# One more expert tile in the ramp, a new order of its work, and router products of 120 columns

## Chip, core and metric

One core of one Trainium2 chip runs one launch of the kernel. The metric is the device time of that launch in microseconds (us); less is better. The engines are named as in the profile: PE (TensorE matmul), PEld (its weight load), DVE (VectorE), ACT (ScalarE), POOL (GpSimd) and SP (SyncE, which issues most DMAs).

## What is computed

x has 2 batches of 2048 tokens of 256 numbers, all float32. After a layer norm, two branches work on the same rows, and their product is added to x:

```python
xn = _layernorm(x, axis=-1)
s = _L0_attn_ref(xn, ...)          # q, k, v, gate: xn @ W; delta rule over 2048 tokens; @ Wo
g = _silu(_L0_ffn_ref(xn, ...))    # 8 experts, each token goes to the one of its largest logit
x = x + s * g

# in the attention branch, 4 heads, keys of 128, values of 64
k = k * rsqrt(sum(k * k) + 1e-12);  beta = sigmoid(xn @ Wb)
delta = (v_t - einsum('bhk,bhkv->bhv', k_t, S)) * b_t;  S = S + k_t delta;  o_t = q_t S
o = o * rsqrt(mean(o * o) + 1e-5) * norm_w * silu(xn @ Wg)
# in the expert branch
logits = xn @ router_w.T;  expert = argmax(softmax(logits))
out = square(relu(xn @ expert_fc[e])) @ expert_proj[e].T
```

## The kernel before

**Tiles.** The tokens of each batch make 16 chunks (c) of 128 rows. One chunk is two row tiles, one of each batch (b = 0, 1), and eight states (2 batches by 4 heads). The attention branch goes chunk by chunk, since the state S is carried on. Its frontend for chunk a is K, Q and VG (products of `xT` with `wk_sb`, `wq_sb`, `wvg_sb`), the transposes kT, the Gram products G and the products PTm. The inverse of a triangular matrix is built in six levels: M0, then for each level l the products L, Dm and T, each waiting on a result that DVE (`Pm_`, `dM`) or ACT (`dZ`) writes from the product before; F and Zc close it. KS, U, O, dS, `ogT_` and `wo` then carry the state through the chunk. Products that need more than float16 are three float16 products of high and low parts (`pairs`).

**Experts.** The rows are sorted by expert into 39 tiles of 128 rows. A tile needs its rows, gathered from `xn_d` in DRAM by POOL (`rows(j)`), and the two weights of its expert (`load_weights(j)`, SP, 2 MB). `experts(n)` issues the next n of a stream of units, 16 to a tile: eight with `fcw` (L461), eight with `pjw` (L472), and the transposes of the next tile's rows (L444) inside them. Buffers ring over three tiles.

**Routing.** `logits_of(c)` multiplies the chunk by `wbr_sb`, which holds the 4 columns for beta and the 8 of the router: 12 moving columns, four float32 products for a chunk, which the trace shows as 8 matmuls. Chunks 0 and 1 (EARLY) go to one bank, the rest to another. When all 16 chunks have logits, ACT copies them (`logits_rest`), DVE makes one-hots of them (`choose`, `count`), PE ranks them (`ranks`, L402 and L404, and `counts`), DVE pads the counts (`pad_counts`), PE adds offsets (`places`), DVE turns that into places (`place_rows`), and into one-hots of rows and of tiles (`tiles_onehot`, `rows_onehot(0)`, `rows_onehot(1)`, `tile_numbers`, and `tile_rows` on ACT), PE multiplies these (`tokens_of_rows`, L431), and DVE writes `from_row` and `to_row` (`keep_tokens`). `past_tiles`, `experts_of_tiles` and `keep_experts` name each tile's expert, `tile_e`; SP waits for that before the first expert weights (L328) and for `keep_tokens` before the third.

**Order.** Each engine runs its own list, written out by hand, in order; semaphores join them. There is a ramp, 14 steps and a tail. The ramp normalises x (loads in five parts, X_PARTS; `stats_of`, `variance` on DVE, `rstd_of` on POOL, `normal` on ACT and DVE), transposes it (`turn(c)` on PE, `keep_xT(c)` on ACT), routes, does the frontend of chunks 0 and 1, the levels of chunk 0 and FIRST_TILES expert tiles. Step i does the recurrence of chunk i-1, the levels of chunk i and the frontend of chunk i+1, with three expert tiles (`step3`) or two (`step2`); STEPS lists them. PE's ramp begins with 64 products of zeros (`warm_up`, L372). A step begins on PE with KS, and on DVE with `R32` (L1518). The tail does the last two tiles and chunk 15, multiplies by the experts' output and adds x.

Of the kernel before, what the change touches and what calls it, by code (L numbers as in the profile page):

```python
# [29 lines left out]
P = 128  # L30
# [36 lines left out]
def build_program(nc, x, wq, wk, wvg, wbr, wo, norm_w, fc, pj, out):  # L67
    with ExitStack() as ctx:
# [19 lines left out]
        FIRST_TILES, STEPS = 1, [3] * 8 + [2] * 6  # L88
# [199 lines left out]
        with nc.Block() as block:  # L288
            @block.sync
            def _(sp):  # L290
# [12 lines left out]
                load_w(wbr_sb, wbr, wbr_in)  # L303
                load_w(wk_sb, wk, wk_in)
                load_x(1)
                load_w(wq_sb, wq, wq_in)
                load_w(wvg_sb, wvg, wvg_in)
                for k in range(2, len(X_PARTS)):
                    load_x(k)
# [50 lines left out]
            def _(pe):  # L360
# [26 lines left out]
                def logits_of(c):  # L387
                    pe.wait_ge(xT_ok, c + 1)
                    if c == 0:
                        pe.wait_ge(wbr_in, 16)  # L390
                    for b in range(B):
                        o = lg_first[:, 2 * c + b, :] if c < EARLY else lg_rest[:, 2 * (c - EARLY) + b, :]
                        for k in range(KC):
                            ins = pe.matmul(o, xT[:, c, b, k, :], wbr_sb[:, k, :], start=(k == 0), stop=(k == KC - 1))  # L394
                    ins.then_inc(lgp, 1)

# [283 lines left out]
                def ramp():  # L680
# [3 lines left out]
                    logits_of(0)  # L684
                    logits_of(1)
                    turn(2)
                    turn(3)
                    K(0, 0)
                    logits_of(2)
                    logits_of(3)  # L690
                    Q(0, 0)
                    turn(4)
                    turn(5)
                    K(0, 1)
# [7 lines left out]
                    Q(0, 1)  # L702
                    logits_of(7)
                    logits_of(8)
                    turn(10)
                    turn(11)
                    logits_of(9)
                    turn(12)
                    VG(0, 0)
                    logits_of(10)  # L710
                    turn(13)
                    logits_of(11)
                    turn(14)
                    logits_of(12)
                    logits_of(13)
                    turn(15)
                    kT(0, 0)
                    logits_of(14)
                    logits_of(15)
                    G(0, 0)  # L720
                    kT(0, 1)
                    PTm(0, 0)
                    VG(0, 1)
                    G(0, 1)
                    ranks()
                    counts()
                    M0(0)
                    places()
                    Q(1, 0)
                    L(0, 0)  # L730
                    K(1, 0)
                    Dm(0, 0)
                    Q(1, 1)
# [39 lines left out]
                    PTm(1, 0)  # L773
                    experts(3)
# [164 lines left out]
            def _(act):  # L939
# [121 lines left out]
                def ramp():  # L1061
                    normal(0)
                    normal(1)
                    keep_xT(0)
                    normal(2)
                    keep_xT(1)
                    normal(3)
                    keep_xT(2)
                    keep_xT(3)
                    ksq_(0, 0)  # L1070
                    logits_first()
                    normal(4)
# [7 lines left out]
                    ksq_(0, 1)  # L1080
# [8 lines left out]
                    q_h(0, 1)  # L1089
# [14 lines left out]
                    M0c(0, 0)  # L1104
                    M0c(0, 1)
                    q_h(1, 0)
                    dZ(0, 0, 0)
                    q_h(1, 1)
                    dZ(0, 0, 1)
                    tile_rows()  # L1110
# [23 lines left out]
                    dZf_(0, 1)
                    keep_y(0)
                    y_sigmoid(0)
                    keep_rows(1)
# [136 lines left out]
            def _(dve):  # L1274
# [309 lines left out]
                def ramp():  # L1584
# [4 lines left out]
                    normal(1)  # L1589
# [602 lines left out]
```

## Time and profile before

| | us |
|---|---|
| three timed runs | 813.15, 813.34, 815.94 |
| their median | 813.34 |
| the profiled execution, its own time | 815.19 |
| span of the profiled execution, first to last instruction | 813.4 |
| PE busy in that span | 773.4 (95%) |
| PE weight loads | 655.9 (81%) |
| DVE, POOL, ACT busy | 529.8, 391.0, 346.9 |
| mean granted clock of PE | 0.966 |

The profiled time is 1.8 us more than its span. All times of rows count from the start of the span. A timeline row gives start, duration, engine, line, operation, the tiles written and read, the shape, and how many instructions are merged in it (xN); in brackets stands the idle time before it and who ended it. Matmuls are pipelined, so the start of the next row, not the duration, tells what a group of them took.

### The profile page before, as it was taken

To read this page: it belongs to the slowest core of one execution; us is meant where nothing else is said; L and a number is where in the kernel's file an instruction comes from. 1 tells how busy PE (TensorE), PEld (TensorE's weight loads), DVE (VectorE), ACT (ScalarE), POOL (GpSimd) and SP (SyncE) were. 2 spreads that over 40 slices of the span, in tenths; PEclk is the share of its full clock that TensorE was granted. 3 is DMA by queue.
4 is the path that set the end of the run, shared out by engine and by line. 5 is a ranking of instruction groups with operands and counts; after the bars stand their busy time and mean duration, and the time that the engine had idled before them with its cause. 6 is when DMAs were issued, how large, how long until landed. Compare 5 with 4: busy or idle time off the path is not lost.

```text
span 813.4 us, 22106 instructions
## 1 busy us (share of the span) xinstructions
PE 773.4 (95%) x8970; PEld 655.9 (81%) x8970; DVE 529.8 (65%) x1159; ACT 346.9 (43%) x754; POOL 391.0 (48%) x407
## 2 busy tenths in 40 slices
PE   6997899999999999999999999999999999999953
PEld 5874788888888889888888888878787878788842
DVE  5568575655756556575665746776767676777587
ACT  3823334444443445344444444444443534344420
POOL 5512473545626364363544625463647464554421
PEclk9969899999999999999999999999999999999965
DMA  9505534424343263333533343232333323140087
GB/s 299 197 11 222 213 118 166 186 112 164 135 170 125 111 212 139 118 124 145 206 112 130 135 175 147 112 124 112 124 111 118 118 110 127 62 172 10 21 275 249
DMA packets 37748, 116.25 MB, mean 143 GB/s; under 512 B 3664, under 2 KB 24400, under 8 KB 27664
## 3 DMA queue, kind: packets, MB, share of 16 engines
q1 hardware_dynamic: 33904, 104.62, 35.3%
q0 software_dynamic: 3744, 10.23, 3.9%
q8 instruction: 72, 1.18, 0.6%
q14 instruction: 28, 0.23, 0.1%
HBM read 101.33 MB, written 13.50 MB: 141 GB/s over the span
## 4 chain that ended last, share of the span: by engine, by line
PE 88%; DVE 4%; POOL 3%; DMA 2%; issue 2%; ACT 1%; another core or an unknown queue 1%; POOLq 0%; DVEq 0%; SPq 0%
PE bank L461 18%; PE bank L472 16%; PE bank L505 7%; PE bank L537 7%; PE bank L490 7%; PE bank L435 4%; PE bank L437 4%; PE bank L436 4%; PE bank L676 4%; PE bank L572 3%; PE bank L582 3%; PE bank L592 2%; PE bank L517 2%; POOL ImM L2043 2%; PE bank L394 2%
## 5 line engine op out<-in xcount | busy, mean ns | idle before, releaser
L472 PE MATMUL bank<-wts,hT 128*128 128x256 f32 x624 | 173.0, 394 | 0.0
L461 PE MATMUL bank<-xsT,wts 128*128 128x128 f32 x1248 | 167.9, 282 | 0.2
L461 PEld LDWEIGHTS bank<-xsT,wts 128*128 128x128 f32 x1248 | 151.8, 193 | 11.0 <-issue 11.0
L1495 DVE TENSOR_TENSOR Pm<-bank,lvl_mask 128x256 f16<-128x256 f32 x192 | 72.6, 419 | 70.4 <-PE bank L572 69.4
L1038 ACT CAST Z<-bank 128x256 f16<-128x256 f32 x192 | 63.5, 376 | 120.8 <-PE bank L592 120.7
L2024 POOL TENSOR_TENSOR XTl<-f_t,XTh 128x512 f16<-128x512 f32 x32 | 40.1, 1261 | 154.7 <-DVE XTh L1438 154.7
L472 PEld LDWEIGHTS bank<-wts,hT 128*128 128x128 f32 x624 | 104.7, 191 | 6.8
L1506 DVE TENSOR_TENSOR M<-bank,M 128x256 f16<-128x256 f32 x192 | 73.4, 418 | 56.3 <-PE bank L582 54.9
L982 ACT ACTIVATE hT<-bank 128x512 f32<-128x512 f32 x78 | 46.7, 598 | 51.3 <-PE bank L461 51.0
L537 PE MATMUL bank<-wvg_sb,xT 128*128 128x512 f32 x128 | 65.1, 633 | 0.3 <-DVE gate L1457 0.3
L505 PE MATMUL bank<-xT,wq_sb 128*128 128x128 f32 x512 | 64.0, 279 | 0.0
L490 PE MATMUL bank<-wk_sb,xT 128*128 128x512 f32 x128 | 62.3, 609 | 0.0
L505 PEld LDWEIGHTS bank<-xT,wq_sb 128*128 128x128 f32 x512 | 61.1, 194 | 0.4
L2043 POOL TENSOR_TENSOR ImM<-ident,M 128x512 f32<-128x512 f16 x32 | 38.1, 1212 | 45.4 <-DVE M L1506 45.4
L582 PEld LDWEIGHTS bank<-Pm,Z 128*128 128x128 f16 x768 | 35.2, 99 | 24.3 <-issue 13.1
L1997 POOL TENSOR_TENSOR y_sb<-y_sb,y_sg 128x256 f32<-128x256 f32 x39 | 29.7, 763 | 48.3 <-ACT y_sg L1001 48.1
L986 ACT ACTIVATE hT<-hT 128x512 f32<-128x512 f32 x78 | 49.3, 633 | 1.1
L2018 POOL TENSOR_TENSOR k16l<-f_t,k16h 128x512 f16<-128x512 f32 x32 | 38.1, 1206 | 24.0 <-DVE k16h L1424 24.0
L1431 DVE TENSOR_TENSOR f_t<-bank,up_neg 128x512 f32<-128x512 f32 x32 | 21.9, 684 | 39.6 <-PE bank L437 39.2
L592 PEld LDWEIGHTS bank<-ident,M 128*128 128x128 f16 x768 | 35.1, 99 | 14.3 <-DVE M L1506 4.0
L1477 DVE COPY M<-ident 128x512 f16<-128x512 f16 x32 | 21.0, 656 | 38.0 <-PE bank L437 34.0
L2001 POOL DMA_INDIRECT y_d<-y_sb,to_row x39 | 41.6, 1066 | 8.7 <-issue 5.3
(213 smaller groups left out, 1957.7 us busy)
## 6 DMA issues: line engine op xcount, KB each, us to landing
wts<-in_fc SPq DMA_DIRECT2D x39, 1024.0 KB
wts<-in_pj SPq DMA_DIRECT2D x39, 1024.0 KB
wts<-in_x SPq DMA_DIRECT2D x10, 512.0 KB, 9.6
wts<-y_d SPq DMA_DIRECT2D x4, 1024.0 KB, 9.2
out_x<-wts SPq DMA_DIRECT2D x16, 256.0 KB, 2.3
xn_d<-wts SPq DMA_DIRECT2D x3, 1024.0 KB, 4.4
x_first<-in_x SPq DMA_DIRECT2D x4, 512.0 KB, 12.1
wts<-in_x SPq DMA_DIRECT2D x4, 256.0 KB, 4.0
```

Of the source, the lines that this page charges most:

```text
L461: ins = pe.matmul(psum[bank[n]][:, (c % 4) * P:(c % 4 + 1) * P], fcw[r][:, k, c * P:(c + 1) * P], xsT[:, k, :], start=(k == 0), stop=(k == ...
L472: ins = pe.matmul(psum[bank[0]][:, 0:D], hT[:, c, :], pjw[r][:, c, :], start=(c == 0), stop=(c == HC - 1))
L490: ins = pe.matmul(psum[KG_BANK[b]][:], xT[:, a, b, k, :], wk_sb[:, k, :], start=(k == 0), stop=(k == KC - 1))
L505: ins = pe.matmul(bank4(QV_BANK)[:, h, :], wq_sb[:, k, h * DK:(h + 1) * DK], xT[:, a, b, k, :], start=(k == 0), stop=(k == KC - 1))
L537: ins = pe.matmul(psum[QV_BANK][:], xT[:, a, b, k, :], wvg_sb[:, k, :], start=(k == 0), stop=(k == KC - 1))
L582: ins = pe.matmul(half4(b)[:, h, :], Z[:, H * b + h, :], Pm[:, H * b + h, :], start=True, stop=True)
L592: ins = pe.matmul(half4(b)[:, h, :].rearrange("p (n c) -> p n c", c=s), M[:, H * b + h, :], evens(ident16[:].unsqueeze(1), s, 1)[:, 0], st ...
L986: act.activation(half(n), half(n), ACT.Square).then_inc(sq_ok[n], 1)
L1038: act.copy(evens(h4(Z, b), s, 1), half4(b).rearrange("p h (n c) -> p h n c", c=s)).then_inc(dZ_ok[b], 1)
L1495: dve.tensor_tensor(h4(Pm, b).rearrange("p h (n c) -> p h n c", c=s), half4(b).rearrange("p h (n c) -> p h n c", c=s), mask, ALU.mult).the ...
L1506: dve.tensor_tensor(evens(h4(M, b), s), half4(b).rearrange("p h (n c) -> p h n c", c=s), evens(h4(M, b), s), ALU.add).then_inc(dM_ok[b], 1)
L2043: pool.tensor_tensor(h4(ImM, b), ident16[:].unsqueeze(1).to_broadcast([P, H, P]), h4(M, b), ALU.subtract).then_inc(ImM_ok[b], 1)
```

## The change

The lists of PE, ACT, DVE and POOL in the ramp are written anew; `step3`, `step2`, the tail and all other operations stay as they are. The ramp issues two expert tiles instead of one, and one of the three-tile steps becomes a two-tile step. Parts 1 to 4 of x move ahead in SP's queue: part 1 ahead of `wk`, parts 2 and 3 ahead of `wq`, part 4 ahead of `wvg`. A router product streams the 12 columns of `wbr_sb` ten times, as a broadcast, and writes 120 columns of its bank, of which the first 12 are kept; the 108 others are written over by later chunks or not read.

The diff, without indentation in the lists of calls; what is cut moves the rest of the frontend of chunk 1 and of the levels of chunk 0 on ACT, DVE and POOL to match the list of PE, which is whole.

```diff
--- before.py
+++ after.py
@@ -85,7 +85,7 @@
         EARLY = 2
         WARM_UP = 64
         X_PARTS = [range(0, 2), range(2, 4), range(4, 8), range(8, 12), range(12, 16)]
-        FIRST_TILES, STEPS = 1, [3] * 8 + [2] * 6
+        FIRST_TILES, STEPS = 2, [3] * 7 + [2] * 7
         assert FIRST_TILES + sum(STEPS) + 2 == NT
 
 
@@ -301,12 +301,13 @@
         load_x(0)
         load_w(wbr_sb, wbr, wbr_in)
+        load_x(1)
         load_w(wk_sb, wk, wk_in)
-        load_x(1)
+        load_x(2)
+        load_x(3)
         load_w(wq_sb, wq, wq_in)
+        load_x(4)
         load_w(wvg_sb, wvg, wvg_in)
-        for k in range(2, len(X_PARTS)):
-            load_x(k)
         load_w(wo_sb, wo, wo_in)
         sp.dma_start(nw_sb[:], norm_w).then_inc(wo_in, 16)
         xn_v = xn_d.rearrange("(q p) d -> p q d", p=P)
@@ -389,10 +390,14 @@
             if c == 0:
                 pe.wait_ge(wbr_in, 16)
             for b in range(B):
-                o = lg_first[:, 2 * c + b, :] if c < EARLY else lg_rest[:, 2 * (c - EARLY) + b, :]
+                bank, q = (RANK_BANK, 2 * c + b) if c < EARLY else (LG_BANK, 2 * (c - EARLY) + b)
+                o = psum[bank][:, q * (H + E):(q + 10) * (H + E)].rearrange("p (r n) -> p r n", r=10)
                 for k in range(KC):
-                    ins = pe.matmul(o, xT[:, c, b, k, :], wbr_sb[:, k, :], start=(k == 0), stop=(k == KC - 1))
+                    ins = pe.matmul(o, xT[:, c, b, k, :], wbr_sb[:, k, :].unsqueeze(1).to_broadcast([P, 10, H + E]),
+                                    start=(k == 0), stop=(k == KC - 1))
             ins.then_inc(lgp, 1)
         def ranks():
             pe.wait_ge(consts, C_ROUTE)
@@ -682,16 +687,16 @@
 turn(0)
 turn(1)
 logits_of(0)
+K(0, 1)
 logits_of(1)
 turn(2)
+K(0, 0)
 turn(3)
-K(0, 0)
+Q(0, 0)
+turn(4)
 logits_of(2)
 logits_of(3)
-Q(0, 0)
-turn(4)
 turn(5)
-K(0, 1)
 logits_of(4)
 turn(6)
 turn(7)
@@ -699,79 +704,79 @@
 turn(8)
 logits_of(6)
 turn(9)
-Q(0, 1)
 logits_of(7)
 logits_of(8)
 turn(10)
+logits_of(9)
+kT(0, 1)
+kT(0, 0)
 turn(11)
-logits_of(9)
 turn(12)
-VG(0, 0)
+turn(13)
 logits_of(10)
-turn(13)
+turn(14)
 logits_of(11)
-turn(14)
+G(0, 1)
+G(0, 0)
+turn(15)
 logits_of(12)
 logits_of(13)
-turn(15)
-kT(0, 0)
 logits_of(14)
 logits_of(15)
-G(0, 0)
-kT(0, 1)
+Q(0, 1)
 PTm(0, 0)
-VG(0, 1)
-G(0, 1)
 ranks()
 counts()
+places()
+K(1, 0)
+VG(0, 0)
+PTm(0, 1)
 M0(0)
-places()
-Q(1, 0)
 L(0, 0)
-K(1, 0)
+tokens_of_rows()
+experts_of_tiles()
 Dm(0, 0)
-Q(1, 1)
+VG(0, 1)
 T(0, 0)
 L(0, 1)
 Dm(0, 1)
-experts_of_tiles()
+Q(1, 0)
 T(0, 1)
+K(1, 1)
+L(0, 2)
+transpose_rows(0)
+Q(1, 1)
+experts(1)
+Dm(0, 2)
+experts(5)
+T(0, 2)
+experts(4)
+L(0, 3)
+experts(2)
+kT(1, 0)
+Dm(0, 3)
+experts(4)
+T(0, 3)
 VG(1, 0)
-PTm(0, 1)
-L(0, 2)
-tokens_of_rows()
-Dm(0, 2)
-VG(1, 1)
-T(0, 2)
-K(1, 1)
-L(0, 3)
-Dm(0, 3)
-transpose_rows(0)
-T(0, 3)
-experts(1)
-L(0, 4)
-experts(2)
-Dm(0, 4)
-experts(2)
-T(0, 4)
-experts(2)
-L(0, 5)
-experts(2)
-Dm(0, 5)
 experts(1)
 kT(1, 1)
+L(0, 4)
+experts(3)
+Dm(0, 4)
+G(1, 0)
+G(1, 1)
+T(0, 4)
+experts(3)
+L(0, 5)
+experts(4)
+Dm(0, 5)
+VG(1, 1)
 T(0, 5)
-experts(1)
-kT(1, 0)
+PTm(1, 0)
+PTm(1, 1)
 F(0)
-G(1, 1)
-experts(1)
-G(1, 0)
+experts(5)
 Zc(0)
-PTm(1, 1)
-experts(1)
-PTm(1, 0)
-experts(3)
@@ -1062,22 +1067,21 @@
 normal(0)
 normal(1)
 keep_xT(0)
+keep_xT(1)
 normal(2)
-keep_xT(1)
 normal(3)
+ksq_(0, 1)
 keep_xT(2)
-keep_xT(3)
-ksq_(0, 0)
 logits_first()
 normal(4)
+ksq_(0, 0)
 normal(5)
-q_h(0, 0)
+keep_xT(3)
+normal(6)
 keep_xT(4)
-normal(6)
-keep_xT(5)
...
@@ -1086,55 +1090,63 @@
 normal(11)
 keep_xT(9)
 normal(12)
-q_h(0, 1)
 normal(13)
 normal(14)
 keep_xT(10)
 keep_xT(11)
+normal(15)
+kTc(0, 1)
+kTc(0, 0)
 keep_xT(12)
-sig(0, 0)
-normal(15)
 keep_xT(13)
+q_h(0, 0)
 keep_xT(14)
 keep_xT(15)
-kTc(0, 0)
 logits_rest()
-kTc(0, 1)
+q_h(0, 1)
+sig(0, 0)
+M0c(0, 0)
+ksq_(1, 0)
+tile_rows()
+M0c(0, 1)
+weigh_wo()
...
@@ -1586,107 +1598,107 @@
 stats_of(0, 0)
 stats_of(0, 1)
 variance(0)
-normal(1)
 stats_of(1, 0)
 stats_of(1, 1)
 variance(1)
-normal(3)
+normal(1)
 stats_of(2, 0)
 stats_of(2, 1)
 variance(2)
+normal(3)
 stats_of(3, 0)
 stats_of(3, 1)
 variance(3)
 normal(5)
+kss_(0, 1)
+stats_of(4, 0)
 normal(7)
-stats_of(4, 0)
 kss_(0, 0)
 normal(9)
 stats_of(4, 1)
 variance(4)
+f_t(0, 1)
+f_t(0, 0)
+k_h(0, 1)
 normal(11)
+k_h(0, 0)
+normal(13)
+normal(15)
+X32(0, 1)
+X32(0, 0)
 q_l(0, 0)
-kss_(0, 1)
-normal(13)
-f_t(0, 1)
+X_h(0, 1)
+MZ(0, 1)
+X_h(0, 0)
+MZ(0, 0)
+choose()
+P32(0, 0)
 q_l(0, 1)
-k_h(0, 1)
-normal(15)
-f_t(0, 0)
+count()
+P_h(0, 0)
+pad_counts()
+Zo(0, 0)
+Zo(0, 1)
+place_rows()
+tiles_onehot()
+rows_onehot(0)
+tile_numbers()
+rows_onehot(1)
+Pm_(0, 0, 1)
 v(0, 0)
-k_h(0, 0)
+past_tiles()
+Pm_(0, 0, 0)
 gate_(0, 0)
-X32(0, 0)
-choose()
-X_h(0, 0)
-count()
-MZ(0, 0)
-X32(0, 1)
-Zo(0, 0)
-X_h(0, 1)
-v(0, 1)
-MZ(0, 1)
-pad_counts()
-Zo(0, 1)
-gate_(0, 1)
-P32(0, 0)
-place_rows()
-Pm_(0, 0, 0)
-Pm_(0, 0, 1)
-q_l(1, 0)
-tiles_onehot()
+keep_tokens()
+keep_experts()
 dM(0, 0, 0)
 dM(0, 0, 1)
-rows_onehot(0)
+v(0, 1)
+gate_(0, 1)
 Pm_(0, 1, 0)
-past_tiles()
 Pm_(0, 1, 1)
-q_l(1, 1)
 dM(0, 1, 0)
-keep_experts()
 dM(0, 1, 1)
-rows_onehot(1)
-tile_numbers()
+P32(0, 1)
+P_h(0, 1)
+q_l(1, 0)
...
@@ -2064,43 +2076,46 @@
 first_consts()
+rstd_of(0)
 root_consts()
-rstd_of(0)
+rstd_of(1)
 route_consts()
-rstd_of(1)
+rstd_of(2)
+rstd_of(3)
+first_root()
+krn_(0)
+rstd_of(4)
+k_l(0, 1)
+k_l(0, 0)
 level_consts(0)
 level_consts(1)
 level_consts(2)
 level_consts(3)
-rstd_of(2)
-rstd_of(3)
-first_root()
-rstd_of(4)
-krn_(0)
 level_consts(4)
 level_consts(5)
-k_l(0, 1)
-k_l(0, 0)
+X_l(0, 0)
 row_consts()
-X_l(0, 0)
-root_(0)
 X_l(0, 1)
 P_l(0, 0)
 rows(0)
+root_(0)
 P_l(0, 1)
 rows(1)
+krn_(1)
+k_l(1, 0)
 rows(2)
...
```

## Rows read from the trace of the kernel before

**Rows 1.** The page, 40 equal slices: PE busy and PE's granted clock, in tenths.
```profile
PE   6997899999999999999999999999999999999953
PEclk9969899999999999999999999999999999999965
```
**Rows 2.** Windows of the ramp: stretch, length, busy us (instructions) by engine, clock, DMA.
```profile
11.40:40.60 29.20, 28.24 (x221) 24.71 (x219) 17.93 (x62) 20.89 (x43) 18.34 (x33) 1.00 0.74 243
40.60:50.90 10.30, 10.30 (x64) 8.95 (x64) 3.72 (x9) 3.21 (x5) 0.53 (x1) 0.50 0.08 24
50.90:57.70 6.80, 5.44 (x66) 4.43 (x65) 6.26 (x18) 1.27 (x3) 1.75 (x2) 1.00 0.00 0
...
81.60:88.40 6.80, 4.20 (x30) 3.94 (x31) 0.76 (x2) 0.92 (x3) 2.38 (x4) 0.50 1.01 393
```
**Rows 3.** Timeline of DVE: the first instruction of steps 2, 3, 10 and 11.
```profile
150.81 0.69 DVE L1518 TENSOR_TENSOR ru<-v_sb,bank 128x512 f32<-128x512 f32 x1 [1.06 <-PE bank L437]
199.93 0.69 DVE L1518 TENSOR_TENSOR ru<-v_sb,bank 128x512 f32<-128x512 f32 x1 [1.06 <-PE bank L437]
...
537.71 0.69 DVE L1518 TENSOR_TENSOR ru<-v_sb,bank 128x512 f32<-128x512 f32 x1 [0.59 <-PE bank L437]
580.24 0.69 DVE L1518 TENSOR_TENSOR ru<-v_sb,bank 128x512 f32<-128x512 f32 x1 [0.59 <-PE bank L437]
```
**Rows 4.** Windows: one step with three tiles, one with two; columns as in rows 2.
```profile
148.00:197.10 49.10, 49.08 (x573) 42.11 (x571) 29.49 (x64) 21.90 (x48) 24.19 (x25) 1.00 0.40 146
540.00:582.50 42.50, 42.16 (x521) 35.32 (x520) 30.49 (x64) 18.65 (x41) 23.06 (x22) 1.00 0.30 113
```
**Rows 5.** Timeline of PE in the ramp: logits, transposes, K and Q at full clock.
```profile
22.83 1.88 PE L490 MATMUL bank<-wk_sb,xT 128*128 128x512 f32 x4
24.55 0.96 PE L394 MATMUL bank<-wbr_sb,xT 128*128 128x12 f32 x8
...
26.27 0.96 PE L394 MATMUL bank<-wbr_sb,xT 128*128 128x12 f32 x8
27.08 0.63 PE L383 MATMUL bank<-ident,wts 128*128 128x128 f32 x4
...
28.83 1.95 PE L505 MATMUL bank<-xT,wq_sb 128*128 128x128 f32 x16
30.62 1.85 PE L394 MATMUL bank<-wbr_sb,xT 128*128 128x12 f32 x16
```
**Rows 6.** Timeline of PE: the logits of chunks 14 and 15.
```profile
42.13 3.53 PE L394 MATMUL bank<-wbr_sb,xT 128*128 128x12 f32 x16
```
**Rows 7.** Timeline of PE: start of G(1,1), twelve float16 products, and what follows.
```profile
95.41 0.22 PE L435 MATMUL bank<-kT 128*128 128x128 f16 x1
...
96.08 0.65 PE L472 MATMUL bank<-wts,hT 128*128 128x256 f32 x2
```
**Rows 8.** Timeline of DVE: choose begins, rows_onehot(0), tile_numbers, keep_tokens ends.
```profile
47.65 0.41 DVE L1341 TENSOR_REDUCE top<-wts 128x32 f32<-128x256 f32 x1
...
63.28 2.28 DVE L1382 TENSOR_TENSOR wts<-numbers,pos_l 128x2048 f16<-128x2048 f16 x1
...
70.21 1.44 DVE L1394 TENSOR_TENSOR wts<-wts,numbers 128x1248 f16<-128x1248 f16 x1
...
76.56 0.19 DVE L1404 SCALAR_TENSOR_TENSOR to_row<-token,empty 128x39 int32<-128x39 f32 x1
```
**Rows 9.** Timeline: first expert weights (SP), first gather (POOL), first transposed rows (PE).
```profile
68.82 0.36 SPq L321 DMA_DIRECT2D wts<-in_fc  x1
...
77.06 1.22 POOL L1988 DMA_INDIRECT xs<-xn_d,from_row  x1 [1.78 <-DVE to_row L1404]
...
84.08 0.69 PE L444 MATMUL bank<-ident,xs 128*128 128x128 f32 x2 [4.38 <-DMA xs<-xn_d,from_row]
```
**Rows 10.** Timeline of PE: the first expert unit and the start of step 1 (KS).
```profile
85.32 1.19 PE L461 MATMUL bank<-xsT,wts 128*128 128x128 f32 x4
...
101.08 0.19 PE L435 MATMUL bank<-S_h,kT 128*128 128x64 f16 x1
```

More of the change, by code:

```diff
@@ L1064, in ramp @@
                     keep_xT(0)
+                    keep_xT(1)
                     normal(2)
-                    keep_xT(1)
                     normal(3)
+                    ksq_(0, 1)
                     keep_xT(2)
-                    keep_xT(3)
-                    ksq_(0, 0)
                     logits_first()
                     normal(4)
+                    ksq_(0, 0)
                     normal(5)
-                    q_h(0, 0)
+                    keep_xT(3)
+                    normal(6)
                     keep_xT(4)
-                    normal(6)
-                    keep_xT(5)
                     normal(7)
                     normal(8)
-                    ksq_(0, 1)
+                    keep_xT(5)
                     keep_xT(6)
@@ L1103, in ramp @@
+                    M0c(0, 0)
[3 more added lines that the diff above has]
+                    weigh_wo()
                     sig(0, 1)
-                    M0c(0, 0)
-                    M0c(0, 1)
+                    dZ(0, 0, 0)
+                    dZ(0, 0, 1)
                     q_h(1, 0)
[L1107 to L1110, printed above, removed]
                     dZ(0, 1, 0)
@@ L1112, in ramp @@
                     dZ(0, 1, 1)
-                    sig(1, 0)
-                    weigh_wo()
-                    ksq_(1, 0)
+                    ksq_(1, 1)
+                    keep_rows(0)
+                    relu(0, 0)
+                    sq(0, 0)
                     dZ(0, 2, 1)
                     dZ(0, 2, 0)
-                    sig(1, 1)
-                    ksq_(1, 1)
-                    keep_rows(0)
+                    relu(0, 1)
+                    sq(0, 1)
+                    q_h(1, 1)
@@ L1121, in ramp @@
+                    keep_rows(1)
+                    kTc(1, 0)
                     dZ(0, 3, 0)
                     dZ(0, 3, 1)
-                    relu(0, 0)
+                    sig(1, 0)
+                    kTc(1, 1)
+                    keep_y(0)
+                    y_sigmoid(0)
+                    relu(1, 0)
+                    sq(1, 0)
                     dZ(0, 4, 0)
                     dZ(0, 4, 1)
-                    sq(0, 0)
-                    relu(0, 1)
+                    relu(1, 1)
@@ L1128, in ramp @@
                     dZ(0, 5, 0)
                     dZ(0, 5, 1)
-                    kTc(1, 1)
-                    kTc(1, 0)
-                    sq(0, 1)
+                    sq(1, 1)
+                    sig(1, 1)
+                    keep_y(1)
+                    dZf_(0, 1)
                     dZf_(0, 0)
[L1134 to L1137, printed above, removed]
+                    keep_rows(2)
+                    y_sigmoid(1)
@@ L1641, in ramp @@
+                    gate_(0, 1)
                     Pm_(0, 1, 0)
-                    past_tiles()
                     Pm_(0, 1, 1)
-                    q_l(1, 1)
                     dM(0, 1, 0)
-                    keep_experts()
                     dM(0, 1, 1)
-                    rows_onehot(1)
-                    tile_numbers()
+                    P32(0, 1)
+                    P_h(0, 1)
+                    q_l(1, 0)
+                    kss_(1, 0)
                     Pm_(0, 2, 0)
+                    kss_(1, 1)
@@ L1651, in ramp @@
                     Pm_(0, 2, 1)
-                    v(1, 0)
-                    P_h(0, 0)
-                    gate_(1, 0)
-                    P32(0, 1)
+                    dM(0, 2, 1)
                     dM(0, 2, 0)
-                    dM(0, 2, 1)
-                    keep_tokens()
-                    kss_(1, 0)
-                    P_h(0, 1)
-                    v(1, 1)
+                    f_t(1, 0)
+                    k_h(1, 0)
+                    f_t(1, 1)
                     Pm_(0, 3, 0)
@@ L1663, in ramp @@
                     Pm_(0, 3, 1)
+                    k_h(1, 1)
+                    q_l(1, 1)
+                    dM(0, 3, 1)
                     dM(0, 3, 0)
-                    dM(0, 3, 1)
-                    kss_(1, 1)
                     Pm_(0, 4, 0)
@@ L1670, in ramp @@
                     dM(0, 4, 1)
-                    f_t(1, 1)
-                    f_t(1, 0)
-                    k_h(1, 1)
+                    X32(1, 1)
+                    v(1, 0)
+                    gate_(1, 0)
                     Pm_(0, 5, 0)
                     Pm_(0, 5, 1)
-                    k_h(1, 0)
-                    dM(0, 5, 0)
-                    dM(0, 5, 1)
-                    Fr_(0, 0)
-                    Fr_(0, 1)
-                    X32(1, 1)
                     X_h(1, 1)
                     X32(1, 0)
+                    dM(0, 5, 0)
                     X_h(1, 0)
+                    dM(0, 5, 1)
+                    v(1, 1)
+                    Fr_(0, 1)
+                    Fr_(0, 0)
+                    P32(1, 0)
                     P32(1, 1)
-                    P32(1, 0)
+                    gate_(1, 1)
                     P_h(1, 1)
                     P_h(1, 0)
-                    gate_(1, 1)
                 def step3(i, t):
@@ L2089, in ramp @@
                     rows(0)
+                    root_(0)
                     P_l(0, 1)
                     rows(1)
+                    krn_(1)
+                    k_l(1, 0)
                     rows(2)
-                    krn_(1)
                     k_l(1, 1)
-                    k_l(1, 0)
+                    X_l(1, 1)
                     ImM_(0, 0)
+                    gate_y(0)
                     ImM_(0, 1)
-                    X_l(1, 1)
                     X_l(1, 0)
-                    gate_y(0)
+                    P_l(1, 1)
+                    gate_y(1)
+                    rows(3)
                     send_y(0)
+                    send_y(1)
                     P_l(1, 0)
-                    P_l(1, 1)
                     root_(1)
```

## Prediction

> **What bounds the kernel now.** I read the page's slices first. PE is busy in nine tenths or more of nearly every slice from the fifth on, at full clock; the ramp (the first five slices, up to 101 us) and the tail are the exceptions [rows 1]. A three-tile step takes 199.93 - 150.81 = 49.12 us with PE busy 49.08 of 49.10; a two-tile step takes 580.24 - 537.71 = 42.53 us with 42.16 of 42.50 [rows 3, 4]. So the steps are bound by PE and their lists don't change: the sum is about the ramp and about one step that becomes shorter. The ramp ends for PE with the first KS, at 101.08 [rows 10]. Windows cut where the granted clock changes show two kinds of loss there [rows 2]: PE at the lower level (1.2 GHz instead of 2.4), from 40.6 to 50.9, when it was never idle, and again after the hole at 80; and PE waiting, 84.08 - 4.38 = 79.7 to 84.08 for the gather of the first tile's rows [rows 9]. That wait is the last piece of one long chain: last logits at 45.66 [rows 6], choose at 47.65, `to_row` at 76.75 [rows 8], gather issued at 77.06, first expert unit at 85.32 [rows 9, 10]. Until that unit PE has only the frontends and levels, and spends them while it waits.
>
> **The tile moved into the ramp.** One tile is worth 49.08 - 42.16 = 6.9 us of PE [rows 4]. The ramp gets 6.9 longer, and the steps 49.12 - 42.53 = 6.6 shorter [rows 3]: net +0.3. By itself it brings nothing; it gives the ramp work once weights and rows are there.
>
> **The logit products.** 16 chunks, four float32 products each. With 12 columns a chunk takes 27.08 - 26.27 = 0.81, or 0.20 a product [rows 5]. Ten times the columns would be ten times the time if streaming were what they wait for. But Q, eight products of 128 columns, takes 30.62 - 28.83 = 1.79, or 0.22 a product, with a new weight load for each as well [rows 5]. 120 columns can't cost more than these 128: the added cost is between 0 and 64 x 0.02 = 1.3 us, and I take 0.6, as 120 lies next to 128 but below it. Broadcast float32 columns don't occur in this trace; were the ten repeats read at half pace, 64 x 0.2 = 12.8 would be added, a rival below. What it buys is the clock: the fall at 40.6 came in a stretch in which PE was busy, 28.24 of 29.20 [rows 2], with logits and transposes alone around it. The logits of the last two chunks then took 3.53 instead of 1.6 [rows 5, 6], and half of the stretch from 40.6 to 42.13, 0.8, was lost before them. I take 2.7 as given back before the last logit.
>
> **Work ahead of the last logit.** PE's list there loses one Q (1.79) and one VG (1.72, as K: 24.55 - 22.83 [rows 5]) and gains kT(0,1) and both G. Twelve float16 products take 96.08 - 95.41 = 0.67 [rows 7], so G is 0.67, and kT with eight 0.45: +1.8. Last logit: 45.66 - 3.5 + 1.8 - 2.7 + 0.6 = 41.9, and 41.5 with the small waits for `xT` at the start (0.96 of the first 29.2 us were idle [rows 2]), of which K(0,1) now fills some. x must allow this: part 2 comes 1 MB and part 4 half a MB earlier in SP's queue, `wk` half a MB later, `wq` 1.5 MB and `wvg` 2.5 MB later. At 243 GB/s and more [rows 2] half a MB is 2 us at most; Q(0,0) and VG(0,0) stand far enough behind (VG now after the route's first part), so the moved weights cost nothing, unless `wk` lands after the first logits, which are among PE's first work. ACT gets kTc before the last `keep_xT`, some 2 us, with the transposes ahead of it; I put the bound of that at +1.
>
> **The route chain.** Before, choose to `to_row` took 76.75 - 47.65 = 29.1 [rows 8], of which the 26 routing instructions of DVE between these rows, start to start, are 14.6 (five of choose 2.2, count 0.5, three of pad_counts 0.7, seven of place_rows 2.6, tiles_onehot 1.4, two rows_onehot 4.5, tile_numbers 1.4, six of keep_tokens 1.2). The rest is levels and frontend put between, and waits for PE. The new list has almost nothing between them. The chain: 14.6, less 0.5 for count (beside ranks), plus ranks and counts on PE 2.1, places 0.3, tokens_of_rows 1.2, Zo 0.7, and the few blocks ahead of keep_tokens 0.5: 18.9. Choose can begin 0.5 after the last logit, at 42.0, if DVE is done with X and MZ, which it should be at 41. So `to_row` is at 60.9 instead of 76.75. The added wait is on PE: tokens_of_rows now stands ahead of Dm(0,0) and everything after, and DVE holds Pm(0,0) back until its one-hots are made. PE's cover between ranks and tokens is K, VG, PTm, M0 and L, some 4.5 us, against 11.5 of DVE: a hole of about 6 us (53 to 59), which didn't exist.
>
> **From there to the first expert unit.** The weights are no longer ahead: `tile_e` is written just after `to_row`, so SP issues them at 61.2 instead of 68.82. 2 MB at 393 GB/s [rows 2] are 5.3: there at 67 to 68. The gather took 84.08 - 77.06 = 7.0 among weight traffic [rows 9]: there at 68. PE meanwhile has VG(0,1), Q(1,0), K(1,1), Q(1,1), 7.0 by the pitches above, and the products of levels 0 to 2, seven groups of 0.22: 8.5, from 59.7, plus 1.5 of waits for DVE and ACT between them: 69.7 at full clock. The clock will not be full: the hole of 4.4 us brought the lower level from 81.6 to 88.4, until 4.3 us after work resumed [rows 2, 9]. The new hole is longer. Bounds: nothing, and all 8.5 of work at half pace; nearest is the row of the old hole, so I take 3.0. The first expert unit is at 72.7, and neither weights nor rows are late.
>
> **From there to KS.** Before: 101.08 - 85.32 = 15.8 [rows 10]. New in this part: five level groups, 1.1; VG(1,0) and VG(1,1), 3.4; the tile, counted above. Gone: half pace from 85.32 to 88.4, -1.5. Waits of the second tile on its chain (relu, square, the other bank) get 0.5.
>
> **Sum.** First unit 72.7 - 85.3 = -12.6; +1.1 + 3.4 - 1.5 + 0.5 = +3.5; tile +0.3: **-8.8 us**. The profiled execution would go from 815.19 to 806.4; against the median, 813.34 - 8.8 = **804.5**.
>
> **Rivals.** (a) The clock stays low for longer. The hole, then level products with short waits between them: if PE runs at half pace from 59 until the first expert unit, +5.5 more; with a late start of the second tile's chain +1: -2.3, 811. For it: the old ramp fell four times. Against it: four large float32 products stand in that part. Chance 0.12.
>
> (b) Transposes don't hold the clock. The fall at 40.6 came after a stretch in which transposes alternate with logits [rows 2]; either could be to blame. In the new list kT(0,1), kT(0,0) and turns 11 to 14 stand together with the logits of two chunks alone among them. A fall there would put G, the last turn, four logits, Q, PTm and ranks, 7.5 us of work, at half pace, less what the route's start hides: +4.5, -4.3, 809.0. Chance 0.10. The Trainium skill says in "TensorE: Matmul & The Clock Gate", part 4, that transposes don't count as activity for the clock gate in the way products do; no row here parts them from narrow products.
>
> (c) Better: full clock from 59 on, and logits at no cost: -8.8 - 3.6 - 1 = -13.4, 800.0. Chance 0.12.
>
> (d) The route isn't earlier, because DVE and ACT are late with the frontend and choose starts where it did: then only the cut from 29.1 to 18.9 is left but the old cover is too, first unit at 78 and more: -3, 810.3. Chance 0.06.
>
> (e) Slower: the logit products cost ten times their columns in full, 12.8 (broadcast read at half pace, or weight loads no longer beside them). All of it lies before choose and on the chain: -8.8 + 12.8 = +4.0, 817.3. It decides from about 9 us of added cost. Against it are Q's 128 columns at 0.22. Chance 0.04. That the change does nothing (the 12-column rows kept the clock low only by accident) is inside (b).
>
> Forecast -8.8 (-6 to -12): 0.56. **Range**: the bounds of the clock term (3.6 down, 5.5 up) and of the logits give 800.0 to 811.0; it holds the forecast, (b), most of (a) and (d). 0.5% is 4.1 us, about what a measurement of this kernel can tell from no change. Faster by more than that: 0.56 and (c)'s 0.12, with 0.05 of (b), 0.04 of (a) and 0.02 of (d): 0.79. Slower by more: 0.03 of (e). Between them: 0.18.
>
> **What would show it.** In the new trace: the first fall of the clock not before the last logit, and that logit near 41.5; a chunk's logits 0.81 to 0.90 apart; `to_row` near 61; PE idle 5 to 7 us before L431, and no longer wait before L444; first L461 near 73; KS near 98.9; steps of 49.1 and 42.5, seven each; the tail as before. I am wrong if the clock is low beyond 66, if L444 or L461 waits for a DMA, or if a step's length changes.

## Result and the profile after

The changed kernel takes 806.31 us (median of four; 805.54 to 806.95) against 813.73 of the kernel before (the three runs above and one of 814.12): ratio 0.9902, 95% interval 0.9888 to 0.9916, so 6.8 to 9.1 us faster (the two medians alone give 0.9909, 7.4 us). Forecast was 804.5 in a range of 800.0 to 811.0. The profiled spans differ by more, 813.4 to 803.8, because executions of the kernel before scatter: 811.2 to 815.9 in 23 of them beside the first experiments, and one of 808.45 among 12 beside the second. The changed kernel's stay within 805.3 and 807.0. One execution of the kernel before beside the last experiments took 1974.76 us, a slow one, and is counted nowhere.

The slices of the page, as rows 1:

```profile
PE   6969999999999999999999999999999999999953
PEclk9999999999999999999999999999999999999955
```

The clock is at nine tenths or more in all of the ramp's five slices; before it was down to 6 in the third and to 8 in the fifth. Windows cut at the changes of the clock, as rows 2:

```profile
9.20:57.00 47.80, 41.20 (x391) 36.13 (x389) 37.86 (x104) 28.04 (x57) 24.64 (x47) 1.00 0.51 172
57.00:60.40 3.40, 3.12 (x42) 3.00 (x43) 2.07 (x10) 0.00 (x0) 0.00 (x0) 0.50 0.02 5
60.40:70.60 10.20, 9.32 (x82) 6.59 (x81) 7.17 (x19) 2.92 (x8) 5.79 (x6) 1.00 0.72 275
70.60:84.20 13.60, 13.59 (x134) 11.86 (x135) 5.58 (x13) 7.07 (x15) 4.73 (x5) 1.00 1.03 395
```

One fall of 3.4 us is left in the ramp where there were four, of 23.9 us. PE lacks 6.6 us of busy time from 9.2 to 57.0, and none after the first expert unit, although the DMA engines are busy all the way from 70.6 to 84.2 (share 1.03). The chain from the logits, timelines of PE, DVE, POOL and SP (as rows 6, 8, 9, 10). The line numbers have moved: L397 is the former L394, L436 L431, L440 L435, L449 L444 and L466 L461.

```profile
36.74 3.73 PE L397 MATMUL bank<-wbr_sb,xT 128*128 128x120 f32 x32
...
41.05 0.42 DVE L1353 TENSOR_REDUCE top<-wts 128x32 f32<-128x256 f32 x1 [1.06 <-ACT wts L970]
...
51.17 2.28 DVE L1394 TENSOR_TENSOR wts<-numbers,pos_l 128x2048 f16<-128x2048 f16 x1
53.37 1.46 DVE L1406 TENSOR_TENSOR wts<-wts,numbers 128x1248 f16<-128x1248 f16 x1
54.74 2.28 DVE L1394 TENSOR_TENSOR wts<-numbers,pos_l 128x2048 f16<-128x2048 f16 x1
...
57.28 2.24 PE L436 MATMUL bank<-wts 128*128 128x78 f16 x32 [2.29 <-DVE wts L1394]
...
60.70 0.19 DVE L1416 SCALAR_TENSOR_TENSOR to_row<-token,empty 128x39 int32<-128x39 f32 x1
...
61.20 1.22 POOL L2000 DMA_INDIRECT xs<-xn_d,from_row  x1 [14.24 <-DVE to_row L1416]
...
62.05 0.36 SPq L322 DMA_DIRECT2D wts<-in_fc  x1
...
68.38 0.41 PE L449 MATMUL bank<-ident,xs 128*128 128x128 f32 x2
...
70.61 0.71 PE L466 MATMUL bank<-xsT,wts 128*128 128x128 f32 x4
...
96.91 0.19 PE L440 MATMUL bank<-S_h,kT 128*128 128x64 f16 x1
...
146.77 0.19 PE L440 MATMUL bank<-S_h,kT 128*128 128x64 f16 x1
```

The last logit is done at 40.5 (45.7 before). DVE makes its one-hots one right behind the other. PE waits for them at L436, and no longer for the gathered rows at L449, where it used to wait 4.4 us. The time ahead of L436 in which PE has little it may do is called the hole below. What PE waits for in the ramp once its warm-up runs, the waits above 0.2 us (total us, times, longest):

```profile
PE bank L436 <- DVE wts L1394: 2.3, 1, 2.3
PE bank L577 <- ACT M L1037: 2.1, 2, 1.7
PE bank L419 <- DVE padded L1368: 1.3, 1, 1.3
PE bank L407 <- DVE onehot L1357: 0.9, 1, 0.9
PE bank L577 <- ACT Z L1043: 0.6, 1, 0.6
```

The steps have the old lengths, one window of each kind, as rows 4:

```profile
148.60:197.70 49.10, 49.07 (x571) 42.11 (x571) 29.47 (x65) 21.88 (x48) 24.15 (x25) 1.00 0.40 147
528.00:570.50 42.50, 42.16 (x522) 35.30 (x522) 30.49 (x64) 18.62 (x42) 23.06 (x21) 1.00 0.31 113
```

### The profile page after: what moved, and what is told of

It reads as the page before. It is cut to its first block, busy times and chain, and to the rows that moved or that the text cites. A ratio compares the mean times of both kernels' runs of the same rounds, so it can differ in the third digit from the quotient of the medians.

```text
span 803.8 us, 22106 instructions
## 1 busy us (share of the span) xinstructions
PE 764.4 (95%) x8970; PEld 649.3 (81%) x8970; DVE 531.9 (66%) x1159; ACT 345.8 (43%) x754; POOL 393.3 (49%) x407
## 4 chain that ended last, share of the span: by engine, by line
PE 88%; DVE 5%; POOL 3%; issue 2%; DMA 1%; another core or an unknown queue 1%; ACT 1%; DVEq 0%; POOLq 0%; SPq 0%
PE bank L466 18%; PE bank L477 16%; PE bank L542 7%; PE bank L510 7%; PE bank L495 6%; PE bank L442 4%; PE bank L440 4%; PE bank L441 4%; PE bank L681 4%; PE bank L577 3%; PE bank L587 3%; PE bank L597 2%; POOL ImM L2055 2%; PE bank L397 2%; PE bank L522 2%
## 5 line engine op out<-in xcount | busy, mean ns | idle before, releaser
L466 PE MATMUL bank<-xsT,wts 128*128 128x128 f32 x1248 | 167.1, 281 | 0.1
L466 PEld LDWEIGHTS bank<-xsT,wts 128*128 128x128 f32 x1248 | 150.8, 192 | 10.9 <-issue 10.7
L1518 DVE TENSOR_TENSOR M<-bank,M 128x256 f16<-128x256 f32 x192 | 73.3, 418 | 58.2 <-PE bank L587 57.5
L542 PE MATMUL bank<-wvg_sb,xT 128*128 128x512 f32 x128 | 62.9, 614 | 0.0
L2000 POOL DMA_INDIRECT xs<-xn_d,from_row x39 | 40.9, 1048 | 20.3 <-DVE to_row L1416 14.2
L2030 POOL TENSOR_TENSOR k16l<-f_t,k16h 128x512 f16<-128x512 f32 x32 | 38.3, 1213 | 15.7 <-DVE k16h L1436 15.7
```

Of the source, the lines that this page charges most:

```text
L466: ins = pe.matmul(psum[bank[n]][:, (c % 4) * P:(c % 4 + 1) * P], fcw[r][:, k, c * P:(c + 1) * P], xsT[:, k, :], start=(k == 0), stop=(k == ...
L542: ins = pe.matmul(psum[QV_BANK][:], xT[:, a, b, k, :], wvg_sb[:, k, :], start=(k == 0), stop=(k == KC - 1))
L1518: dve.tensor_tensor(evens(h4(M, b), s), half4(b).rearrange("p h (n c) -> p h n c", c=s), evens(h4(M, b), s), ALU.add).then_inc(dM_ok[b], 1)
```

## Experiments

The theory: the gain is the route chain, shorter in its list and started earlier; the wide products keep the clock up in front of it; the second tile fills what follows. Each run was timed against the kernel before on the same chip; medians and ratios are given. As the kernel before scatters by 4 us, ratios of different groups of runs are rough to 0.2%; between groups I compare the medians of the kernels with wide products, whose executions mostly agree within 1.5 us. Four ran together first.

**The changed kernel again.** 

> The changed kernel again, as the anchor for the runs beside it. If the profiled execution of the kernel before was one of its longer ones (815.19 against a median of 813.7), the ratio stays near 0.990 (806 us) and the profile of the kernel before on this chip should have another pattern of low clock in its ramp. If the 9.6 us between the two profiled spans are the true size, the ratio goes to 0.988.


Measured 805.74, the kernel before 814.25 (23 executions): 0.9896 (0.9876 to 0.9917), -8.5 us. The profile had the same pattern, one low stretch of 3.4 us. The kernel before ranges over 4.7 us, and its mean granted clock over 0.965 to 0.974, the higher in the shorter executions. So its profile, with 0.966, was one of the longer ones, and the ratio came out as first expected. The other half of that expectation, another pattern of low clock in a second profile of the kernel before, has no trace to it.

**12 columns in the new order.**

```diff
-o = psum[bank][:, q * (H + E):(q + 10) * (H + E)].rearrange("p (r n) -> p r n", r=10)
+o = psum[bank][:, q * (H + E):(q + 1) * (H + E)]
...
-    ins = pe.matmul(o, xT[:, c, b, k, :], wbr_sb[:, k, :].unsqueeze(1).to_broadcast([P, 10, H + E]),
+    ins = pe.matmul(o, xT[:, c, b, k, :], wbr_sb[:, k, :],
```

> The changed kernel with router products of 12 columns again, all lists as changed. My theory: narrow products and transposes let the clock fall before the last logit, as in the kernel before at 40.6; the last logit comes at 42 to 44 instead of 40.5, and the time is 2 to 3 us above the changed kernel (about 808.5). Rival: the new order keeps the clock up by itself, since G, kT and Q stand elsewhere: then the narrow products are 64 x 0.02 = 1 us cheaper and the time is equal to the changed kernel's or up to 1 us less.


Measured 810.14 with a range of 807.65 to 816.37, 0.9967 (0.9942 to 0.9992): 4.4 us above the changed kernel by medians, 5.6 by means (811.4 against 805.9). The profiled execution, among the long ones (span 814.6), shows where; windows of its ramp:

```profile
9.20:25.00 15.80, 15.56 (x126) 13.36 (x125) 12.24 (x46) 10.89 (x24) 9.59 (x20) 1.00 0.99 338
25.00:42.10 17.10, 17.10 (x94) 17.10 (x92) 5.63 (x15) 9.68 (x18) 10.23 (x21) 0.50 0.35 116
```

PE ran at 1.2 GHz for 17.1 us without one idle moment, on narrow logits and transposes. Choose began at 49.8 instead of 41.05. The effect is larger than I said, and it is a lottery: four of the twelve executions lie within 0.5 us of 807.7, five are above 813.

**120 columns in the old order.** The same edit of the product, put into the kernel before. 

> The kernel before with only its router products made 120 columns wide. My theory: no fall of the clock at 40.6, last logit at 43.5 to 44 instead of 45.66, and as the chain from there to the gather is DVE's, the 2 us come through: 811 to 812. Rival: the chain waits elsewhere (PE's own list after the logits), and nothing or under 0.5 us comes through: 813.5. If wide products cost their columns in full, 12 us more: 825.


Measured 812.72 (811.36 to 813.7), 0.9977 (0.9965 to 0.9989): -1.5. No fall at 40.6; the last logit ends at 43.5 and choose begins at 44.9, 2.7 earlier than at 47.65, and `to_row` is 4 us earlier. Of that the first expert unit, at 82.39, keeps 2.9, and KS, at 99.16, 1.9: PE waits longer for the gather than before,

```profile
PE bank L446 <- DMA xs<-xn_d,from_row: 5.6, 1, 5.6
```

and the hole brings the clock down from 77.4 to 87.6 (before from 81.6 to 88.4). The wide products alone give 1.5, all the rest (order, tile and loads) without them 4.1; together they give 8.5. The rest is worth 7.0 when the clock doesn't fall in front of the chain and 4.1 when it can.

**Loads in their old order.**

```diff
-load_x(1)
 load_w(wk_sb, wk, wk_in)
-load_x(2)
-load_x(3)
+load_x(1)
 load_w(wq_sb, wq, wq_in)
-load_x(4)
 load_w(wvg_sb, wvg, wvg_in)
+for k in range(2, len(X_PARTS)):
+    load_x(k)
```

> The changed kernel with the loads in their old order (part 1 of x behind wk, parts 2 to 4 behind wq and wvg). My theory from the trace of after: DVE waits 0.8 and 2.4 us for parts 1 and 2 even in the new order, so the old one makes these waits 1 to 2 us longer, but PE has spare work until turn 15 and ACT is the one it waits for: 0.5 to 1.5 us slower than the changed kernel (807 to 808). Rival 1: nothing, because the POOL powers of the parts set the pace. Rival 2: the whole delay of 2 us and more comes through, 808.5 or above.


Measured 807.35, 0.9919 (0.9902 to 0.9936): +1.6, just above the 0.5 to 1.5 that I gave. DVE waits 4.9 us for parts of x instead of 3.2, and choose, `to_row` and the first unit are 1.5 us later in the profiles. 0.9 of that is there at the first logit (13.28 against 12.39), a mark that differs by as much between profiles of the changed kernel itself. So the medians show a price of the old order, and the traces give about half of it a place.

The next four ran together, beside a kernel before of 813.14 (808.45 to 815.21).

**One tile in the ramp.** FIRST_TILES 1, eight three-tile steps; the last 16 units and the second tile's work leave the ramp:

```diff
-FIRST_TILES, STEPS = 2, [3] * 7 + [2] * 7
+FIRST_TILES, STEPS = 1, [3] * 8 + [2] * 6
...
 VG(1, 0)
-experts(1)
 kT(1, 1)
 L(0, 4)
-experts(3)
 Dm(0, 4)
...
 T(0, 4)
-experts(3)
 L(0, 5)
-experts(4)
 Dm(0, 5)
...
 F(0)
-experts(5)
 Zc(0)
```

> The changed kernel with one expert tile in its ramp and eight three-tile steps, as before: the 16 units after T(0,3) and the second tile's work on ACT and POOL leave the ramp. My prediction said the tile by itself brings nothing (6.9 us more ramp, 6.6 less steps) but gives work. First unit at 70.6 as in the changed kernel. My theory: 19 us of other PE work remain behind it, and four levels with their answers from DVE and ACT fit into that with 1 to 2 us of new waits: 806.5 to 808. Rival 1: the levels fit without waits: 805.5. Rival 2: the levels are bound by their chain as soon as the tile is gone (3 us and more of waits): 809 or above.


Measured 807.53 (806.82 to 808.9): +1.8 against the changed kernel of the first group, as expected (the ratios, across two groups, give more: 0.9939 against 0.9896). From the first unit (71.20) to KS (94.06) it is 22.9 us instead of 26.3: 3.4 less for 6.9 us of work taken away. The waits are those of the levels, from 70 to 95:

```profile
PE bank L618 <- DVE XTl L1512: 1.4, 1, 1.4
PE bank L587 <- DVE Pm L1495: 1.0, 2, 0.6
PE bank L577 <- ACT Z L1038: 0.4, 1, 0.4
```

The work beside the tile is then bound by the answers of DVE and ACT. So the moved tile, whose PE work I had priced at +0.3, brings 1.8 in all, as cover.

**The hole filled with products of zeros.** `fill(14)` before L(0,0) and `fill(38)` before tokens_of_rows, where

```diff
+def fill(n):
+    pe.wait_ge(lg_ok, 2)
+    pe.wait_ge(beta_ok, 2)
+    zeros = S16[0][:, 0:2, :].rearrange("p h n -> p (h n)")
+    for _ in range(n):
+        pe.matmul(psum[LG_BANK][:, 256:256 + P], zeros, zeros, start=True, stop=True)
```

> The changed kernel with 14 products of zeros (float16, 128 columns) between M0 and L(0,0) and 38 more ahead of the products that give the rows, in the hole where PE waits 1.7 and 2.3 us; their result is used by nobody. It measures what the low clock after the hole (57.0 to 60.4) costs. My theory: no low clock there, the 3.4 us of work run at full pace, first expert unit 1 to 1.5 us earlier: 804.5. Rival 1: the route answers (DVE) set the time, not PE, and nothing comes: 805.7. Rival 2: the fill runs over the hole and delays the route: 806 to 807.


Measured 804.95 (803.92 to 805.26): 0.8 to 1.1 us below the changed kernel's 805.74 and 806.03 in the groups before and after, and no low clock in the ramp. These groups ran on different chips, and the ratios to the kernel before (0.9903 here, 0.9896 and 0.9900 there) show no gain; the traces do: from the first logit to the first unit 57.4 us instead of 58.2, 58.4 and 58.5 in the three profiles of the changed kernel. Part of what the clock gives goes into a new wait:

```profile
PE bank L473 <- DMA wts<-in_pj: 0.5, 1, 0.5
```

This is the first tile's weight: SP issues it only when keep_experts, behind keep_tokens, is done.

**Weights early, VG(0,1) in the hole.** On PE experts_of_tiles goes behind VG(0,0) and VG(0,1) ahead of tokens_of_rows; on DVE

```diff
 place_rows()
+past_tiles()
 tiles_onehot()
+v(0, 0)
+gate_(0, 0)
 rows_onehot(0)
+keep_experts()
 tile_numbers()
```

(and they leave their old places). 

> The changed kernel with the experts' numbers made before the rows (past_tiles, experts_of_tiles, keep_experts ahead of the second rows_onehot), so that the first two expert weights start near 54.5 instead of 62.0, and with VG(0,1) in the hole ahead of the products that give the rows (v and gate of VG(0,0) go ahead of the first rows_onehot on DVE, +0.7 us on the route). My theory: PE is full from 57 to 70.6, so what leaves it there (2.0 us of VG) comes through, less the 0.7, until the gathered rows (6 us after to_row, now near 67.5) are waited for: 1 to 1.5 us faster, 804.5. Rival: the gather ends last, among the traffic of the weights, and the 0.7 us later to_row makes it 0.5 us slower: 806.3.


Measured 805.88 (five of six within 0.2): no gain. SP issues at 57.1 instead of 62.05, but VG(0,1) runs in the part of the hole in which the clock is low, timeline of PE:

```profile
56.32 3.55 PE L542 MATMUL bank<-wvg_sb,xT 128*128 128x512 f32 x4
...
62.88 0.62 PE L597 MATMUL bank<-ident,M 128*128 128x64 f16 x8 [1.42 <-DVE M L1518]
```

It takes 3.55 where 1.7 was counted, and T(0,0), no longer covered by it, waits 1.4 for DVE. Both causes were missing in my expectation; the rival's 806.3 is nearer than my 804.5, its reason (the gather: 0.4 of wait) holds only in part.

**60 columns.** The ten repeats become five. 

> The changed kernel with the router's columns streamed five times (60 columns) instead of ten. If the clock follows from how much PE streams in that stretch, half the columns should lie between: some executions with a fall before the last logit, median 806 to 809 and a wide scatter. If any product wider than 12 columns is enough, 805.2 to 805.7 (up to 1 us cheaper, since weight loads alone then set the pace).


Measured 805.39 (804.52 to 806.92), within the scatter of the changed kernel; no fall before the last logit in the profiled execution. The mean granted clock is 0.975 to 0.978 in its six executions, 0.974 to 0.980 in 13 of the changed kernel and 0.964 to 0.974 in the 12 with 12 columns. Five repeats do what ten do. That leaves little room for the transposes as the cause: they are the same in this run, in the one with 12 columns and in the changed kernel, and only the width parts the first from the others.

Three more ran together, the kernel before at 814.6 (812.54 to 815.61).

**Fill, 60 columns, early weights.** The fill as above; experts_of_tiles directly behind K(1,0), past_tiles and keep_experts around tiles_onehot, and on SP

```diff
 load_weights(0)
+sp.wait_ge(rows_in[0], 16)
 load_weights(1)
```

> Against the changed kernel: the products of zeros of the run before (they kept the clock, and PE then waited 0.5 us for the second expert weight), 60 columns, the experts' numbers made in the hole so that the first tile's weights start about 8 us earlier, and the second tile's weights held back until the first gathered rows have landed. My theory: the wait for the weight goes, first unit 1.3 us earlier than in the changed kernel: 804.3. Rival 1: the gathered rows end last now (6 us after their issue) and nothing comes beyond the fill's 0.8: 805.0. Rival 2: the second tile's weights, 7 us later, are waited for: 806 or above.


Measured 803.77 (803.46 to 804.35), 0.9874 (0.9854 to 0.9893): 2.3 below the changed kernel beside it, better than expected. Weights are issued at 52.19, the first unit is at 68.93; the gather, issued at 60.20, is never waited for. Timeline of PE:

```profile
55.17 2.28 PE L381 MATMUL bank<-S_h 128*128 128x128 f16 x38
57.29 1.34 PE L444 MATMUL bank<-wts 128*128 128x78 f16 x32
```

The 32 products of tokens_of_rows take 1.2 us from start to start instead of 2.2. From the first logit to the first unit it is 56.5 us, against 57.8 in the run with 60 columns alone: clock and weights together give 1.3.

**VG(0,1) and Q(1,0) moved as well.** On top of the last: VG(0,1) directly behind M0(0), `fill(32)`, Q(1,0) between Dm(0,0) and T(0,0), v and gate of both VG products earlier on DVE. 

> As the run before, and PE's hole filled with VG(0,1) (v and gate of VG(0,0) ahead of the first rows_onehot) and 32 products of zeros; Q(1,0) goes between Dm(0,0) and T(0,0), its v and gate ahead of keep_tokens on DVE, where that waits for PE. My theory: VG(0,1), which took 3.55 us at half pace in the hole two runs before, takes 1.7 there; PE's list from the rows' product to the first unit is 9 us instead of 11.2, and the gather, with only one tile's weights beside it, lands in under 5 us: first unit 2 to 2.5 us earlier, 803.3. Rival: the levels wait for DVE as soon as the frontend products are gone from between them (1.4 us before T(0,0) in that run): 804.5 to 805.


Measured 805.16 (804.17 to 807.18), 0.9894: 1.4 slower than without, near the rival's 804.5 to 805. VG runs at full pace now, but v and gate of DVE stand on the route: from the first logit to the rows' product it is 46.4 us instead of 44.9, PE waits 1.8 for the one-hots in spite of VG and 32 products, and L, Dm and T wait 0.2 to 0.4 each afterwards. PE's work was moved to where PE was idle, and DVE's part of it to where DVE was not. Which of the two moves costs more isn't parted.

**The changed kernel a third time.** 

> The changed kernel beside the two versions above, on their chip: 805.7, ratio to the kernel before 0.990.


Measured 806.03 (805.76 to 806.45), 0.9900 (0.9883 to 0.9916). Its profile shows the low stretch as 6.8 us, 55.5 to 62.3.

## Why the prediction was right

The sum held, with errors that cancel. Term by term, from the profiled executions:

| term | forecast | measured | from |
|---|---|---|---|
| last logit ends | 41.5 | 40.5 | L397 |
| choose begins | 42.0 | 41.05 | L1353 |
| `to_row` written | 60.9 | 60.9 | L1416 |
| choose to `to_row` | 18.9 | 19.8 | their difference |
| PE idle ahead of the rows' product | 6 | 4.4, in three pieces | L577, L436 |
| low clock after it, cost | 3.0 | 0.8 to 1.3 | the fill, with and without its new wait |
| first expert unit | 72.7 | 70.61 | L466 |
| from there to KS, tile in it | 15.8 + 3.5 + 6.9 = 26.2 | 26.3 | L440 |
| the tile: its PE work, and all that it brings | +0.3 | -1.8 | one tile in the ramp |
| step 1 | 0 | +1.0 | KS to KS, 49.86 against 48.83 |
| the other steps | 49.1, 42.5 | 49.1, 42.5 | windows |

The two numbers for the tile aren't the same quantity: the cover that it gives was in my 26.2, which came out right.

**The logits.** A product of 120 columns costs what Q's row said. The sixteen of the last four chunks (32 matmuls) take 40.30 - 36.74 = 3.56 from start to start, or 0.22 each; the rival with 12.8 us is out. In the old order they brought choose forward by 2.7 us, the number that I took back. In the new order they buy more: 4.4 us of median and nearly all of the scatter. I read one trace, in which the fall came at 40.6; the run with 12 columns shows that it can come at 25.0 and last 17.1 us. By these rows narrow products with transposes between them don't hold the 2.4 GHz level even when PE is never idle.

**Transposes (rival b).** The forecast against it held: with 60 or 120 columns no fall comes before the last logit, with as many transposes as before. The Trainium skill says ("TensorE: Matmul & The Clock Gate", part 4) that a transpose doesn't count as busy in the way a product does. No run here tests it by itself. The changed kernel's longest stretch of transposes alone, 30.54 to 32.74, lies between wide products and brought no fall. The transposes didn't decide the result.

**The loads.** By its place in the queue `wq` comes 2 MB later and `wvg` 3 MB, where I had 1.5 and 2.5. PE waits for neither, as forecast.

**The low clock behind the hole.** This term was mis-sized: I took 3.0 us from the old hole. Here the clock is low from 57.0 to 60.4, with only 0.28 us of waiting in it. Most of it lies over the rows' product itself, which takes 2.2 us from start to start instead of 1.2 at full clock; that is the 0.9 by which choose to `to_row` is longer than forecast. Behind that product, from 59.56 on, it lasts another 0.84 us, which costs some 0.4. That makes about 1.4, an estimate from these rows; the fill gave 0.8 to 1.1 with a new wait of 0.5 in it, and 1.3 once the weights came early. The work behind the product takes 70.61 - 59.56 = 11.05 us instead of 13.0: the clock 2.6 less, the waits 0.7 less, the products 1.3 more. So the first unit came 2.1 early, by two errors one way and one the other. In the third profile of the changed kernel the stretch was 6.8 us long, 2.3 of it idle, and from the first logit to the first unit it took 58.5 us instead of 58.2: 3.4 us more at the lower level cost 0.3. Rival (a), 811, needed the low clock until the first unit; it was over 10.2 and 9.5 us before it in these two profiles.

**Step 1.** Not in my sum: the work left over from a fuller ramp. In step 1 PE waits once:

```profile
PE bank L563 <- DVE Z L1498: 0.8, 1, 0.8
```

PE's other 0.3 is work: 49.10 us of it as in the later steps, where step 1 before had 48.83. The wait comes from DVE's first copy of the levels, which ends 2.2 us after U's last product, at 102.79 (K follows it there), while POOL still does the products and sends of the second tile:

```profile
102.79 1.96 PE L495 MATMUL bank<-wk_sb,xT 128*128 128x512 f32 x4
...
103.63 1.17 POOL L2042 TENSOR_TENSOR PTl<-f_t,PTh 128x512 f16<-128x512 f32 x1
...
104.15 0.82 DVE L1489 COPY M<-ident 128x512 f16<-128x512 f16 x1 [4.00 <-PE bank L442]
...
106.03 0.28 DVE L1489 COPY M<-ident 128x512 f16<-128x512 f16 x1
...
152.85 1.25 DVE L1489 COPY M<-ident 128x512 f16<-128x512 f16 x1 [2.72 <-PE bank L442]
```

A long copy alone isn't the cause: in step 2 it takes 1.25 us and PE doesn't wait, because it starts 0.2 us behind U (done at 152.65). In step 1 it starts 1.4 behind, later than the products that the profile puts its wait down to; what holds it isn't shown. Before, it started 0.2 behind and took 0.29. With one tile in the ramp the step takes 142.89 - 94.06 = 48.83 again, so the second tile's leftovers bring it. The Trainium skill has a rule that bears on it ("SBUF — State Buffer", section "SBUF: two separate sides"): DVE in some modes and POOL take a pair of ports by turns, for a whole instruction. The rows agree in that POOL's L2042 (103.63 to 104.80) lies over the first copy; they don't agree in that the copy at 106.03 took 0.28 with POOL's L1987 (104.75 to 106.57) over it. It was not tried by itself. I had named a change of a step's length as a sign that I am wrong; here it came, in one step of fourteen.

**The size.** Traces give -4.2 (KS), +1.0 (step 1) and -6.6 (a step's tile), together -9.8 for spans of -9.6. Medians give -7.4 and, with more executions, -8.5. The forecast was -8.8. That they lie so close is in part luck. The terms were worked out on a long execution of the kernel before, and against that one the changed kernel gained more, 815.19 - 805.54 = 9.7; taken off a median of shorter ones they gave 804.5, 1.8 below what was measured. Taken out of the changed kernel one by one, the tile costs 1.8, the loads 1.6 and the wide products 4.4. Such prices don't add up to the whole (the wide products alone, in the old order, gave 1.5), and no run has the new order of the lists alone.

## What to carry to other kernels

Price an engine's narrow products by what they do to the clock of what follows, and look at several executions: where the time of one kernel scatters by half a per cent and its granted clock with it, a fall of the clock may be there by chance, and a few wasted columns may be free. When a serial chain across engines ends in a wait, put its steps next to each other in every list and let the bulk work follow; then look for the hole that this makes elsewhere. Fill such a hole only with what brings no work of the chain's own engine with it: zeros gave 0.8 to 1.1 us, while a real product there, with its work on DVE, gave nothing in one run, and two such moves cost 1.4 in another.

## What was not expected of the hardware

- PE fell to 1.2 GHz from 25.0 to 42.1 with 17.10 of 17.10 us busy, when its router products had 12 columns, with transposes between them; with 60 it didn't. Where between 12 and 60 it turns was not tried.
- 120 columns cost 0.22 us a product against 0.20 for 12; Q's 128 plain float32 columns also cost 0.22, so no price of the broadcast itself is seen.
- With 52 products of zeros in the hole no low clock is left in the ramp, and from the first logit to the first unit it took 57.4 us instead of 58.2 to 58.5.
- Two tensor_scalar instructions of DVE, which take about 0.4 us each, took 2.41 us together while POOL ran two subtractions of 128x512 (L2030, 28.10 to 30.60):

```profile
28.34 2.41 DVE L1336 TENSOR_SCALAR wts<-wts,rstd,shift 128x256 f32<-128x256 f32 x2
```
